# The value matmuls of the last token tile, moved behind its query and key projections

## The reference, cut to what matters

```python
q1 = _heads(x @ Wq1, B, S, H, d)
q2 = _heads(x @ Wq2, B, S, H, d)
k1 = _heads(x @ Wk1, B, S, H, d)
k2 = _heads(x @ Wk2, B, S, H, d)
v = _heads(x @ Wv, B, S, H, 2 * d)
...
a1 = jax.nn.softmax(jnp.where(causal, s1, neg_inf), axis=-1)
a2 = jax.nn.softmax(jnp.where(causal, s2, neg_inf), axis=-1)
comb = a1 - lam[None, :, None, None] * a2
out = jnp.einsum('bhqk,bhkv->bhqv', comb, v)
```

## Time and profile before

| | us |
|---|---|
| runs | 1951.15, 1951.88, 1955.1 (median 1951.88) |
| profiled execution | 1954.14, its span 1952.4 |
| TensorE busy | 1866.5 (96%) |
| ScalarE busy | 1416.0 (73%) |
| VectorE busy | 1013.3 (52%) |
| mean granted TensorE clock | 0.979 |

### The profile page before, as it was taken

The page is one execution under the profiler, slowest core; times in us unless marked ns, Lnnn a source line. Parts: engine busy times, 40 slices in busy tenths (PEclk is TensorE's granted clock), DMA queues, the critical chain, the costliest instruction groups (busy, mean ns, idle before and its releaser), DMA issues. The chain is left out here.

```text
span 1952.4 us, 31608 instructions
## 1 busy us (share of the span) xinstructions
PE 1866.5 (96%) x12160; PEld 1071.7 (55%) x12160; DVE 1013.3 (52%) x1947; ACT 1416.0 (73%) x1715; POOL 232.1 (12%) x308
## 2 busy tenths in 40 slices
PE   7997999999999999999999993999999999999996
PEld 6773333333333333333333333788888888888885
DVE  5555655556645655556645613435455454546342
ACT  4446999999999999999999991535444454545442
POOL 3001111211111111211111110000000000000000
PEclk9998999999999999999999995999999999999998
DMA  8777156533664356543664303000110000000000
GB/s 273 243 248 157 25 101 114 103 66 77 114 120 76 72 98 114 96 76 74 114 120 74 63 1 86 1 27 17 33 33 13 33 12 33 13 33 22 1 11 12
DMA packets 130163, 146.34 MB, mean 75 GB/s; under 512 B 74228, under 2 KB 99956, under 8 KB 122356
## 3 DMA queue, kind: packets, MB, share of 16 engines
q1 hardware_dynamic: 129272, 142.53, 33.9%
q10 hardware_dynamic: 720, 1.57, 0.2%
HBM read 101.86 MB, written 39.06 MB: 72 GB/s over the span
## 5 line engine op out<-in xcount | busy, mean ns | idle before, releaser
L848 ACT ACTIVATE attn_probs<-attn_s_ps 128x1024 f32<-128x1024 f32 x1088 | 1001.7, 1133 | 13.8 <-PE attn_s_ps L874 13.3
L894 PE MATMUL attn_sums_ps<-attn_probs,heads_v 128*32 128x512 f32 (+3 forms) x5120 | 587.4, 540 | 0.7 <-POOL attn_probs L829 0.7
L874 PE MATMUL attn_s_ps<-heads_q,heads_k 50*128 50x512 f32 (+3 forms) x2560 | 453.0, 428 | 12.5 <-DVE heads_q L937 12.1
L874 PEld LDWEIGHTS attn_s_ps<-heads_q,heads_k 50*128 50x128 f32 x2560 | 213.8, 185 | 455.1 <-ACT attn_probs L848 410.4
L1387 ACT ACTIVATE split_whole<-split_hid_ps,scales 128x512 f32<-128x512 f32 x128 | 88.3, 690 | 274.5 <-PE split_hid_ps L1301 274.3
L829 POOL TENSOR_SCALAR_AFFINE_SELECT attn_probs<-attn_probs 128x512 f32<-128x512 f32 x256 | 181.3, 720 | 833.2 <-ACT attn_probs L848 833.2
L1301 PE MATMUL split_hid_ps<-split_hid_b,ffn_r 128*128 128x512 f32 x1024 | 240.8, 392 | 0.0
L1301 PE MATMUL split_hid_ps<-split_hid_a,ffn_r 128*128 128x512 f32 x1024 | 238.0, 391 | 0.0
L1301 PEld LDWEIGHTS split_hid_ps<-split_hid_a,ffn_r 128*128 128x128 f32 x1024 | 190.1, 188 | 41.0 <-DVE split_whole L1525 1.0
L1301 PEld LDWEIGHTS split_hid_ps<-split_hid_b,ffn_r 128*128 128x128 f32 x1024 | 189.8, 188 | 38.2
L894 PEld LDWEIGHTS attn_sums_ps<-attn_probs,heads_v 128*32 128x32 f32 x5120 | 107.6, 108 | 174.6 <-issue 141.4
(11 more groups left out here) (125 smaller groups left out, 1622.1 us busy)
## 6 DMA issues: line engine op xcount, KB each, us to landing
heads_q_raw<-qk_raw SPq DMA_DIRECT2D x60, 384.0 KB
heads_k_raw<-qk_raw SPq DMA_DIRECT2D x60, 384.0 KB
qk_raw<-proj_copies SPq DMA_DIRECT2D x64, 256.0 KB, 2.7
values<-proj_v SPq DMA_DIRECT2D x8, 1024.0 KB, 6.9
diffs<-attn_diff SPq DMA_DIRECT2D x32, 256.0 KB, 4.1
split_heads<-diffs SPq DMA_DIRECT2D x8, 1024.0 KB, 5.2
heads_k_raw<-ones SPq DMA_DIRECT2D x60, 128.0 KB
heads_v<-values SPq DMA_DIRECT2D x15, 512.0 KB, 19.4
```

The source lines that it names most:

```text
L848: nc.scalar.activation(weights, side_by_side, ACT.Exp, scale=SCALE).then_inc(exp_done, 1)
L874: last = nc.tensor.matmul(s_ps[(NU * h + n) % SLOTS][:, s, col:col + width], k_sb[u][rows, b * SEQ + j * PARTS:b * SEQ + (j + 1) * PARTS], ...
L894: last = nc.tensor.matmul(sums[c * D:(c + 1) * D, off:TILE], v_sb[u][:, b * KEY_BLOCKS + j, :], probs[k % PROBS][:, b, s, place:place + wi ...
```

## The change: what it does, and the diff

`value_tile` becomes `value_tiles` and returns a list. For the last tile it is empty for m of 0 to 6 and holds all four value groups for m = 7. So in tile 7 TensorE makes the eight query/key groups first and then the four value groups; ScalarE makes the four value copies behind its eighth query/key copy; SyncE issues the value store behind the store of m = 7 in place of behind that of m = 3. GpSimd's list is the same: its copy for tile 7 waits for the same count of value copies. The other seven tiles are as they were, and no instruction is added or removed on any engine.

```diff
-        def value_tile(t, m):
+        def value_tiles(t, m):
+            if t == LAST:
+                return list(range(SUBS)) if m == M_TILES - 1 else []
             s = m - (M_TILES - SUBS) if t == 0 else m
-            return s if 0 <= s < SUBS else None
+            return [s] if 0 <= s < SUBS else []
...
-                    if value_tile(t, m) == SUBS - 1:
+                    if SUBS - 1 in value_tiles(t, m):
                         sp.wait_ge(v_copied, SUBS * t + SUBS)
                         sp.dma_start(values[:, :, bass.ts(t, SUBS), :].rearrange("h p s d -> p h (s d)"),
                                      v_sb[t % 2][:, :, :, :].rearrange("p h s d -> p h (s d)")).then_inc(v_stored[t % 2], 16)
...
-                    s = value_tile(t, m)
-                    if s is not None:
+                    for s in value_tiles(t, m):
                         if s == 0:
                             act.wait_ge(ones_done, 2)
...
-                    s = value_tile(t, m)
-                    if s is not None:
+                    for s in value_tiles(t, m):
                         if t == 0:
                             pe.wait_ge(wv_ready, 1)
```

## The result

| | runs | median us | ratio to before (95% interval) |
|---|---|---|---|
| before | 22 | 1951.26 (1947.96 to 1955.1) | |
| changed | 22 | 1955.01 (1952.05 to 1958.35) | 1.0018 (1.0012 to 1.0024) |

The change makes the kernel slower by 0.18%, 3.5 us. That is inside the range (1949.5 to 1956.5) and within the 0.2% that I called the same, but it is about six times the +0.6 us that I had worked out. The profiled execution took 1955.57 us, its span 1953.8.

A forecast was written before the change was run, and what follows sets the result against it. TensorE bounds tile 7, ScalarE the attention, and the last store's landing the exit between. Issue -1.57 us and landing +2.2 us sum to +0.6 us: 1951.88 + 0.6 = 1952.5 us, range 1949.5 to 1956.5.

The forecast's parts named there:

- TensorE, ScalarE: cost 0.: Tile 7: the same matmul groups and copies in another order, with no added stall; cost 0.
- SyncE's queue, issue 1.57 us earlier.: SyncE, end of tile 7: backlog worked off beside the value matmuls, last store issued at 152.84 in place of 154.41.
- The landing, 4.5 us, +0.6 us in all.: SyncE's end: last store is 1024 KB, landing in 4.5 us in place of 2.3; with the earlier issue, +0.6 us.
- the exit: Between tile 7 and the attention: taken to be bound by the last store's landing, moving by +0.6 us.
- Its reduction was waiting for VectorE's maxima ... The reduction starts behind the copy, at 153.4.: GpSimd, end of tile 7: maxima come earlier, so the reduction starts as its value copy ends, at 153.4.
- the flag, priced at 0: Flag instructions after GpSimd's reduction: done at 154.6, 0.5 us earlier than before and 2.7 us ahead of the landing.
- A sign of being wrong that I had named: End of the stage: the flag's last instruction ending later than the store's landing would show the forecast wrong.
- The smaller kin of the slower rival: GpSimd's reduction: up to 6.1 us getting ready behind the copy, +4.0 us, 1955.9; 0.14 together with the slower rival.
- the slower rivals: End of tile 7: late landing (+4.6 us) or reduction getting ready (+4.0 us); 0.14 for +2 us and more.
- the landing rival: SyncE's wait for value stores: landing 8.5 us in place of 4.5, 1956.5 us; 0.14 together with its kin.
- Behind the exit, 0.6 us late stays late.: Meeting, flag loads, branch and attention follow SyncE's end at the same distance; attention starts and stays 0.6 us late.

The follow-up runs named there:

- e3: Changed kernel with GpSimd's last two steps swapped, reducing the maxima before copying tile 7's values; ratio to before 1.0003 (0.9988 to 1.0017).
- e5: Changed kernel with the last value store cut to 256 KB, other heads' places filled earlier with tile 6's values; ratio to before 1.0025 (1.0012 to 1.0038).
- e4: Kernel before, with only GpSimd's copy of tile 7's values made to wait for ScalarE's last query/key copy; ratio to before 1.0014 (1.0001 to 1.0026).
- e1: Changed kernel plus one unused GpSimd reduction over partitions ahead of the tile loop; ratio to before 1.0004 (0.9992 to 1.0017).
- e8: Changed kernel again, unchanged, timed beside the kernel before; ratio to before 1.0020 (1.0010 to 1.0030).
- e11: Changed kernel with SyncE's last waits moved past the flag's branch; ratio to before 1.0023 (1.0011 to 1.0034).
- e10: Kernel before with SyncE's last waits moved past the flag's branch; ratio to before 0.9991 (0.9979 to 1.0003).
- e7: Kernel before with tile 7's stores of m = 5 and m = 7 issued by ScalarE in place of SyncE; ratio to before 1.0008 (0.9996 to 1.0020).
- e2: Kernel before plus one unused GpSimd reduction over partitions ahead of the tile loop; ratio to before 1.0009 (0.9996 to 1.0022).
- e6: Changed kernel with a last value store of 256 KB and an unused early GpSimd reduction; ratio to before 1.0014 (1.0003 to 1.0025).
- e9: Changed kernel with GpSimd reducing before its last copy and SyncE's last waits moved past the flag's branch; ratio to before 0.9987 (0.9977 to 0.9997).

## Why the prediction was right in its range and wrong in its sum

- *TensorE, ScalarE: cost 0.* Right. Last matmul 16.7 us behind tile 7's start before (151.81 - 135.10) and now (152.84 - 136.13); ScalarE's last copy ends 17.7 us behind it in both.
- *SyncE's queue, issue 1.57 us earlier.* Right: 17.74 us behind the start of tile 7 for 19.31.
- *The landing, 4.5 us, +0.6 us in all.* The landing was 4.5 us, and the store went out when I had it. SyncE's end moved by 1.1 us, from 21.7 to 22.8 us: its last wait began at 158.8, 0.4 us behind the landing (153.87 + 4.5 = 158.4), and before at 156.7 as the landing came (154.41 + 2.3 = 156.7). In e3, where nothing else stands behind it, the exit is 0.67 us above before. But it isn't the end of the changed kernel's stage, as e5 shows.
- *"Its reduction was waiting for VectorE's maxima ... The reduction starts behind the copy, at 153.4."* This is the step that failed. The reduction started 6.01 us behind the copy and the flag, priced at 0, cost 3.0 us of exit; e4 has the cost (3.4 us) with this one thing changed. In the sum it takes the place of the landing: copy 17.8 + 0.3, getting ready 6.0, and 1.4 from the reduction to the meeting make 25.5 us, where the meeting was. A sign of being wrong that I had named came true: the flag's last instruction ended at 161.41, behind the landing at 158.4.
- *The smaller kin of the slower rival* was this very mechanism, with all 6.1 us and +4.0 us (1955.9). Its place was right and its price near: the meeting came 3.5 us later, and the exit grew by 3.0 because TensorE's branch took 3.37 us for 3.79. That the time lies inside the range is luck as far as the sum goes: only the slower rivals reached that high. I gave it, with the landing rival, 0.14, because of the earlier trace rows: the same operation in head 15 started at once. That row could not speak against it, since it is the second such reduction of the run, and e1 shows that only the first one pays.
- The Trainium skill ("GPSIMD Engine Reference", section "Instruction dispatch") states that the first call to a freshly loaded GpSimd kernel pays about 6 us for loading its code, with no instruction in the profile to show for it. The measured 6.01, 6.09 and 5.91 us agree, and so does its being paid once (e1). I hadn't weighed that page. No run here shows what is loaded; that part is the page's.
- *Behind the exit, 0.6 us late stays late.* Right in kind: with an exit 2.9 us longer the attention of e8 took 1030.69 us, for 1030.70 before, and its finish's start 27.86 us, for 27.87.

## What to carry to other kernels

Idle time ahead of an instruction is written on the releaser that came last; it may hide a second wait of nearly the same length, so before a change moves the instruction in front of it, ask what the engine would do with its input already there. A first use of a special operation can't be priced by a later one: look for the first use in the trace, and put it, or an unused one, where the engine is idle anyway. When a stage ends in a meeting of all engines, list the end of every engine's list, not only of the one that is last now. And where the executions of one kernel fall into two groups by their mean granted clock, compare within the groups before a small ratio is read as the change's.

## What the runs showed of the hardware that I had not expected

- GpSimd's first reduction over partitions needs 5.8 to 6.6 us behind the instruction ahead of it, once in a run, and this runs beside an open wait (e3). It was 5.79 us in e5, 6.24 in e11, 6.32 in e10, 6.50 in e7, and 6.58 early in e1 and e2. It does not go by the DMA traffic alone: with 169 GB/s in that stretch it took 6.24 us in e11 and 6.58 in e1, with 316 GB/s at most 6.14 in the kernel before.
- Issuing a small DMA on SyncE took from 0.59 to 1.08 us (three in 1.78 us mostly, in 2.92 in e7, in 3.23 in e6), and taking two stores off its queue did not shorten it (e7).
- TensorE's flag load and branch took 0.49 to 0.54 and 3.3 to 3.8 us with little DMA traffic (6 to 52 GB/s), 1.05 and 4.39 us beside a 1024 KB store (e9).
- The same stretch of the finish takes 24 or 27.9 us, with the granted clock at 1.00 or 0.50 in part of it, from one execution of a kernel to the next (24.14 in the changed kernel's first profile, 27.86 in e8). Two profiles of one kernel can thus differ by more than this change is worth.
